# Earlier slots and tile-by-tile sends in a routed feed-forward stage, with two dense steps moved behind the row tiles

## The reference

```python
def _L1_ffn_ref(x, ln_gamma, ln_beta, router_w, gate_up_w, down_w, shared_gate_up_w, shared_down_w):
    normed = (xt - mu) * jax.lax.rsqrt(var + LN_EPS) * ln_gamma + ln_beta
    probs = jax.nn.softmax(normed @ router_w.T, axis=-1)
    top_v, top_i = jax.lax.top_k(probs, 2)
    gates = jax.nn.softmax(top_v, axis=-1)
    comb = jnp.sum(jax.nn.one_hot(top_i, E) * gates[..., None], axis=1)
    for e in range(E):
        out = out + comb[:, e, None] * _swiglu(normed, gate_up_w[e], down_w[e])
    return out + _swiglu(normed, shared_gate_up_w, shared_down_w)
```

## Time and profile before

| | us |
|---|---|
| median of 3 runs | 321.09 |
| lowest, highest | 319.01, 323.36 |
| the profiled execution's own time | 319.61 |
| its span, first to last instruction | 317.8 |
| PE busy | 268.3 (84%) |
| DVE busy | 236.4 (74%) |
| ACT busy | 204.4 (64%) |
| POOL busy | 158.9 (50%) |
| mean granted TensorE clock | 0.941 |

### The profile page before, as it was taken

One profiled execution on the slowest core, in us unless ns is written; L12 is line 12 of the kernel. 1 busy time (PEld: TensorE's weight loads), 2 busy tenths in 40 slices (PEclk: granted clock), 3 DMA queues, 4 the chain that ended last, 5 costly groups with the idle time before them and its releaser, 6 DMA issues.

```text
span 317.8 us, 7526 instructions
## 1 busy us (share of the span) xinstructions
PE 268.3 (84%) x2406; PEld 201.9 (64%) x2406; DVE 236.4 (74%) x711; ACT 204.4 (64%) x469; POOL 158.9 (50%) x206
## 2 busy tenths in 40 slices
PE   7878986997999797999988853878899999999950
PEld 4553442555677464676766732368799999999940
DVE  3586198857977666788999967998576767677796
ACT  2964799796577588976855543535657575756560
POOL 2624297024622546643024777770047878787531
PEclk9999999899999999999999655879999999999995
DMA  7890003001269999970000011113122223111064
GB/s 211 233 383 10 1 2 132 0 3 19 117 188 185 178 181 180 190 105 0 2 1 24 30 45 40 53 49 88 37 71 68 78 67 87 51 32 33 8 226 132
DMA packets 34612, 28.12 MB, mean 88 GB/s; under 512 B 3072, under 2 KB 32389, under 8 KB 33936
## 3 DMA queue, kind: packets, MB, share of 16 engines
q1 hardware_dynamic: 32192, 23.77, 33.8%
q0 software_dynamic: 2240, 3.72, 3.6%
q10 hardware_dynamic: 144, 0.15, 0.2%
HBM read 14.15 MB, written 14.40 MB: 90 GB/s over the span
## 4 chain that ended last, share of the span: by engine, by line
PE 52%; DVE 30%; ACT 8%; issue 6%; DMA 2%; SPq 1%; POOL 1%; DVEq 0%
PE bank L1195 47%; DVE region_k L912 2%; DVE region_x L1152 2%; DVE top L911 2%; DMA wr<-in 2%; PE bank L1492 1%; DVE bn_raw L870 1%; DVE nm L1001 1%; DVE region_k L1003 1%; DVE x L1141 1%; DVE x L1142 1%; ACT x_hat L540 1%; DVE x L902 1%; PE bank L1419 1%; DVE region_k L969 1%
## 5 line engine op out<-in xcount | busy, mean ns | idle before, releaser
L1177 DVE TENSOR_TENSOR region_k<-region_x,region_k 128x768 f16<-128x768 f32 (+1 forms) x33 | 30.6, 926 | 21.6 <-ACT region_k L714 21.6
L1195 PE MATMUL bank<-w_high,region_k 128*128 (+1 forms) x380 | 37.8, 221 | 6.4 <-DVE x L1171 3.3
L1195 PE MATMUL bank<-w_scaled,w_high 128*128 128x256 f16 x252 | 42.5, 273 | 0.1
L846 POOL DMA_INDIRECT expert_rows<-region_k,slot_dest x22 | 27.1, 1232 | 26.5 <-DVE region_k L1164 19.2
L714 ACT ACTIVATE region_k<-region_x 128x768 f16<-128x768 f32 (+1 forms) x33 | 26.8, 813 | 15.8 <-DVE region_x L1152 13.7
L820 POOL DMA_INDIRECT dispatched_rows<-region_t,slot x28 | 28.8, 1028 | 16.1 <-issue 8.3
L1195 PEld LDWEIGHTS bank<-w_high,region_k 128*128 128x128 f16 x380 | 30.9, 99 | 7.7 <-issue 7.3
L1195 PE MATMUL bank<-w_scaled,w_low 128*128 128x256 f16 x126 | 34.3, 273 | 0.0
L1195 PE MATMUL bank<-w_low,region_k 128*128 (+1 forms) x190 | 34.0, 221 | 0.0
L1152 DVE SCALAR_TENSOR_TENSOR region_x<-bank,region_w 128x768 f32<-128x768 f32 (+1 forms) x33 | 30.4, 920 | 3.2 <-ACT region_w L719 2.2
L1195 PE MATMUL bank<-filler 128*128 128x512 f16 x94 | 26.9, 407 | 3.9 <-DVE region_k L912 2.4
(11 more groups left out here) (242 smaller groups left out, 736.1 us busy)
## 6 DMA issues: line engine op xcount, KB each, us to landing
dispatched_rows<-pad_rows SPq DMA_DIRECT2D x8, 1048.0 KB, 18.8
w_scaled<-in SPq DMA_DIRECT2D x5, 1024.0 KB, 8.0
w_scaled<-dispatched_rows SPq DMA_DIRECT2D x21, 131.0 KB, 2.3
region_q<-expert_rows SPq DMA_DIRECT2D x3, 512.0 KB, 5.0
x<-in SPq DMA_DIRECT2D x4, 256.0 KB, 4.4
region_w<-in SPq DMA_DIRECT2D x2, 512.0 KB, 7.0
out<-x SPq DMA_DIRECT2D x3, 256.0 KB, 2.3
w_scaled<-in SPq DMA_DIRECT2D x1, 704.0 KB, 4.1
```

The lines of the kernel that those rows point to most:

```text
L846: pool.indirect_dma_start(ytok, bass.IndirectOffsetOnAxis(dst[:, n, h:h + 1].bitcast(U32), 0), yv[n % 4][:, h * D:(h + 1) * D], None, boun ...
L1177: dve.tensor_tensor(hsplit[:, v, k:2 * k], hid[:, v, 0:k], hsplit[:, v, 0:k], ALU.subtract).then_inc(hidden_low, 1)
L1195: return pe.matmul(o, l, r, start=start, stop=stop)
```

## The change

Four things, and with them the line numbers of the changed kernel are a few higher than those before (L1135 becomes L1140, L1152 becomes L1157, L1167 becomes L1172, L820 becomes L826).

1. `DENSE_FIRST` goes from 3 to 1: the rows steps are steps 5 to 25 instead of 7 to 27, and seven dense steps follow them instead of five. The 33 steps are the same ones.
2. On DVE the `slots` of the first two groups come directly behind the place where their ranks are made.
3. POOL's sends are four stages of one tile each instead of two of two, and their places move; `rstd2` of the last two groups stands among them.
4. At the end ACT scales tiles 8 to 11 before its last 16-bit copy, tiles 4 to 7 move from DVE to ACT and POOL, DVE sums its four tiles as 1, 2 and 1, and SP's loads and stores come in another order.

```diff
-DENSE_FIRST = 3
+DENSE_FIRST = 1
...
-C_POOL = {"rstd": -4.6, "early_low": -5.3, "low": -0.9, "rstd2": 6.5, "send": 12.5, "send2": 16.1}
+C_POOL = {"rstd": -4.6, "early_low": -5.3, "low": -0.9, "rstd2": 6.5, "send0": 11.3, "send1": 11.32, "send2": 11.34, "send3": 11.36}
...
-            for g in (0, 2, 1, 3):
+            for g in (2, 0, 1, 3):
                 n = slice(*GROUPS[g])
                 eng.dma_start(yk[:, n, :], ytok_v[:, n, :]).then_inc(x_loaded[g], 16)
-            for g, ready, count in ((2, last_added, 2), (0, sum_done, T), (SPARSE, rows_ready, len(STEPS)), (3, last_added, 4),
-                                    (1, sum_done, 2 * T)):
+            for g, ready, count in ((2, last_added, 2), (0, sum_done, T), (1, last_added, 4), (3, last_added, 6),
+                                    (SPARSE, rows_ready, len(STEPS))):
...
+            def gated_rows(g):
+
+                act.wait_ge(gates_done, 1)
+                act.wait_ge(x_loaded[g], 32)
+                for c in range(2):
+                    for t in range(*GROUPS[g]):
+                        last = act.activation(yk[:, t, c * D:(c + 1) * D], yk[:, t, c * D:(c + 1) * D], ACT.Copy,
+                                              scale=gate[:, t, c:c + 1])
+                    last.then_inc(last_gated, 1)
...
+                if s == len(STEPS) - 2:
+                    gated_rows(2)
...
-            for g in (2, 3):
-                act.wait_ge(x_loaded[g], 32)
...
+            gated_rows(1)
+            gated_rows(3)
...
-                elif stage == "send" and g is not None and g < SPARSE:
-                    pool.wait_ge(padded, 16 * (E + 2))
...
-                    send_rows(range(lo, lo + 2))
-                elif stage == "send2" and g is not None and g < SPARSE:
-                    send_rows(range(lo + 2, hi))
+                elif stage[:4] == "send" and g is not None and g < SPARSE and lo + int(stage[4]) < hi:
+                    if stage == "send0":
+                        pool.wait_ge(padded, 16 * (E + 2))
+                        pool.wait_ge(slots_ready, g + 1)
...
+                    send_rows(lo + int(stage[4]))
...
-            for k, (g, c) in enumerate(((2, 0), (2, 1), (3, 0), (3, 1))):
+            for k, (g, c) in enumerate((g, c) for g in (2, 1, 3) for c in range(2)):
...
-                    sum_rows(range(1, 4))
-            dve.wait_ge(x_loaded[1], 32)
-            sum_rows(range(4, 8))
+                    sum_rows(range(1, 3))
+            sum_rows(range(3, 4))
```

More of the change, by code:

```diff
@@ L99 @@
             ("norm2", 15): 21.9, ("high", 15): 22.1, ("turn_out", 15): 22.3}
-C_DVE_AT = {("affine", 13): 20.8, ("low", 13): 21.0, ("route", 11): 21.4, ("slots", 11): 21.6,
+C_DVE_AT = {("slots", 3): 14.25, ("slots", 7): 18.35, ("affine", 13): 20.8, ("low", 13): 21.0, ("route", 11): 21.4, ("slots", 11): 21.6,
             ("affine", 15): 22.0, ("low", 15): 22.1, ("route", 13): 22.2,
             ("route", 15): 22.5, ("slots", 13): 22.9}
-C_POOL_AT = {("rstd2", 13): 19.4, ("rstd2", 15): 21.5, ("send2", 7): 21.6, ("send", 11): 21.7, ("send2", 11): 21.8, ("send", 13): 21.9}
+C_POOL_AT = {("rstd2", 13): 18.5, ("send0", 7): 18.4, ("send1", 7): 18.6, ("send2", 7): 18.7, ("rstd2", 15): 21.3, ("send3", 7): 21.4,
+             **{(f"send{k}", t): t + 10.5 + 0.1 * k for t in (11, 13) for k in range(4)}}
 FILL_LOAD, FILL_NORM, FILL_CROSS, FILL_SELECT, FILL_ROUND = 10, 4, 2, 3, 4
@@ L724, in _ @@
                     act.activation(gone[:, :], gdif[:, :], ACT.Tanh, scale=0.5).then_inc(top2_tanh, 1)
-            act.wait_ge(gates_done, 1)
-            for g in (2, 3):
-                act.wait_ge(x_loaded[g], 32)
-                for c in range(2):
-                    for t in range(*GROUPS[g]):
-                        last = act.activation(yk[:, t, c * D:(c + 1) * D], yk[:, t, c * D:(c + 1) * D], ACT.Copy,
-                                              scale=gate[:, t, c:c + 1])
-                    last.then_inc(last_gated, 1)
+            gated_rows(1)
+            gated_rows(3)
         @block.gpsimd
```

14 lines of the change are left out of this document (6 added, 8 removed).

## The result

The changed kernel takes **323.76 us** (median of 20 runs, 321.27 to 328.22) beside 320.94 of the kernel before (20 runs, 318.91 to 323.36): a ratio of **1.0079, 95% interval 1.0049 to 1.0110**, or 2.5 us more (2.5 = 0.0079 x 320.94). Medians and ranges here are of all runs; the ratios leave out runs that lie more than 1.5% above the fastest of the same kernel, here 4 of the 20. The forecast was 323.7. The profiled execution took 324.04 us, its span is 322.2 where that of before is 317.8: 4.4 more. Where these 4.4 are is read from four landmarks. The first operation of the slots of group one stands at 165.50; in before the same place is 164.71. The last silu of ACT starts at 305.34; in before at 301.94.

A forecast was written before the change was run, and what follows sets the result against it. From 225 us on, PE working without a gap was taken as the bound; the profiled execution's 319.61 + 3.1 (entry) + 1.5 (clock) - 0.5 (end) gave 323.7 us, range 319.0 to 327.0.

The forecast's parts named there:

- the entry: Going into the rows steps, DVE and then PE wait for the first row tile: +3.1 us, bounds 1.7 to 5.5.
- the clock: PE's granted clock falls to half speed behind the wait for the first row tile: +1.5 us, bounds 0 and 1.7.
- the end: Behind the last matmuls, the rearranged scalings, adds, sums and stores finish earlier: -0.5 us, bounds -2.2 and +0.6.
- sends in time: Rival: POOL's last send ends at 208.8, the row tile lands when DVE asks, total 319.1 us; chance 0.08.
- POOL's stand: POOL waits 2.9 us ahead of its ninth send for the slots of group two, losing most of its 3.8 lead.
- sends gain nothing: Rival: POOL's last send still ends at 213.8, a wait for the row tile of 5.5 us, total 326.1; chance 0.10.
- a fall is likelier than not: PE's granted clock probably drops to 1.2 GHz after the wait for the first row tile, costing 1.5 us.
- the clock holds: Rival: PE's clock does not fall in the wait for the first row tile, total 322.2 us; chance 0.24.
- some 4 us: Forecast time PE stands from 213.6 to 218.0, but for one turn, waiting for the first row tile.
- I take it at its 0.96: DVE's last low half (L1177) takes 0.96 us, not held by POOL's add; if held, 0.6 more.
- PE's last `down` (by 310.5 even at 1.2 GHz) is covered: PE's last `down` is done by 310.5, hidden behind DVE's sums and SP's stores, so it adds no time.
- The tail is freer: Rival: DVE's last sums slip between POOL's adds at 0.34 each, last store 2.2 earlier, total 320.5 us; chance 0.18.

The follow-up runs named there:

- e9: Changed kernel plus 22 matmuls of 256 columns nobody reads, 12 ahead of the first row tile's turn on PE and 10 behind it: 325.19 us, ratio 1.0107.
- e10: Changed kernel with ACT's eight scalings of tiles 8 to 11 moved back behind its last copy: 324.23 us, ratio 1.0119.
- e12: Changed kernel plus 46 matmuls of 256 columns nobody reads, on PE ahead of its last `down`: 323.37 us, ratio 1.0100.
- e1: Kernel before with DENSE_FIRST = 1 and nothing else: 328.19 us, ratio 1.0217.
- e4: Changed kernel with the piece of tiles 0 to 3 stored last instead of second: 323.03 us, ratio 1.0047.
- e7: Changed kernel with DVE's sum of the first token tile moved behind the last product's dense result: 324.57 us, ratio 1.0114.
- e5: Changed kernel with PE's `down` of step 3 ahead of the first turn and DVE's first destination made one step later: 325.18 us, ratio 1.0108.
- e8: Kernel before with the new order of slots, norms and sends and one dense step in front, keeping the old end: 322.27 us, ratio 1.0016.
- e13: Kernel before with the new order of slots, norms and sends, plus 5 unread matmuls of 512 columns ahead of the first stage's second transposes: 320.79 us, ratio 1.0029.

## Why the forecast came out, and what in it was wrong

The time is right, at 323.76 against 323.7, but only the mechanism of the entry bears it. The rest is luck, twice. The error in the clock (+1.5 forecast, 0 in the profiled execution) and that in the end (-0.5 forecast, +1.0 measured) cancel. And the forecast added 4.1 us to one execution of 319.61 that lay 1.3 below the median of 20 runs; added to the median of 321.09 that was known then it would have been 325.2. The change itself measured 2.5 us, not 4.1.

**The sends and the entry: right in mechanism, 0.5 to 1.5 too high.** The first send 1.9 behind the slots, POOL's stand, the last send's end and the order of waits are as forecast; the rival "sends in time" fell with POOL's gap, "sends gain nothing" with last sends that end 46.0 to 47.6 behind the slots against 49.1. The entry is +2.6 in the profiled execution and +1.6 in e9, e10 and e12, instead of +3.1. In the profiled execution SP's first read came 1.76 behind the last send where the earlier trace rows had 2.35, 0.6 less, and the last send ended 0.2 later. What it has above the 1.6 of the others are 0.9 of three sends at 205 to 211 us that took 1.20, 1.41 and 1.19 instead of 0.96 in the changed kernel and 0.96 in e10. What slowed them isn't shown.

**The clock, +1.5: right in size, wrong as the usual case.** That was the step "a fall is likelier than not". It fell in the profiles of e1, e4 and e7 and held in those of the changed kernel, e5, e8, e10 and e12 (e9 was filled): the rival "the clock holds" described the usual execution. Part of the error is the length of the wait, "some 4 us". PE stood 2.96 in the changed kernel, 2.0 or less in e8, e10 and e12, and 3.9 and 5.4 in e4 and e1, where the clock fell. The length alone does not decide it, as e7 stood only 1.8 and lost its clock.

**The end, -0.5: wrong, it is +1.0.** Two steps failed. "I take it at its 0.96" (L1177, now L1182): the row showed it alone, and next to POOL's add it took 1.64. Here the rule that the prediction set against it (the Trainium skill, SBUF — State Buffer, "Who interferes with whom": a DVE instruction with two inputs in SBUF and a GpSimd instruction that reads SBUF block each other, the one that comes second waiting) holds, 0.7 by this trace; e8 and e10, where no add runs at that time, show 0.96. And "PE's last `down` (by 310.5 even at 1.2 GHz) is covered": it could start only when DVE had taken the dense result before it, which stood behind two sums held by POOL; it began at 314.23 at a clock of 0.50, and DVE waited 0.53 for it. e7 and e12 each give back 0.65 of this. POOL's adds ended 9.7 behind the last silu, exactly as forecast (311.6 - 301.94); the last sum came 12.26 behind it instead of 11.0. That is 1.3 of the 1.5 by which the end was wrong; the other 0.3 is the span's end behind the last store's issue, 3.0 instead of 2.7, which the sum had as unchanged; the slowest store lands 2.8 after its issue instead of 2.4. The 1.6 of the four stores in a row was right, and it is the largest single cost in the end: e8, with the same last sum and one store behind it, ends 1.9 earlier, and e4 takes 1.1 of it away. "The tail is freer" fell with 1.35 and 1.37.

**The front, 0: +0.8 in this execution.** The clock fell at 12 to 15 us. The sum 317.8 + 0.8 + 2.6 + 1.0 = 322.2 is the profiled span. On the medians the +1.6 to +2.6 of the entry and the +1.0 of the end make 2.6 to 3.6, and 2.5 (1.6 to 3.5) was measured.

## What to carry to other kernels

A step that is moved to the end of a program pays only if what follows it is not the bound there: follow the last result of the slow engine through every instruction queued ahead of it, before calling it covered. A result that the slow engine finishes last should have one store behind it, not four: that order cost more here than all that was won by moving sums. An add on POOL beside two-input work on DVE lengthens the DVE instruction that the chain needs; released behind it, as in e10, the adds let the last sum end 1.1 earlier, though no time here shows that gain. A gain of a microsecond is read from landmarks of the trace that lie between what varies; the median of 6 or 12 runs that spread over 4 us doesn't show it.

## What the runs showed of the hardware that was not expected

- The first 24 us differ most between the profiles. In five of the fourteen one small DMA lands late and holds one ACT instruction for 1.4 to 2.15 us, PE stands for 2.0 to 2.7 us, the granted clock goes to 0.50 for some microseconds, and everything behind is 2.4 us later or more (first slots at 167.5 to 168.6 instead of 163.6 to 165.1). That this makes the spread of one kernel's runs is likely and not shown: there is one trace of each kernel, and e13 did not shrink the spread. Moving that tanh behind the norms was not tried.
- The wait at the entry, cut by one turn of four transposes, is not equally long in each execution. PE stood 5.4 and 3.9 us in two profiles, and the granted clock fell to 0.50 behind it (e1, e4); it stood 1.1 to 3.0 us in five and the clock held (the changed kernel, e5, e8, e10, e12), and 1.8 us in one where it fell (e7). With matmuls in the wait that nobody reads the clock stayed at 1.00 in the two profiles that had them (e9, e12's end).
- ACT's scalings are not lengthened by POOL's adds as DVE's sums are: 0.30 us each in both pieces, the eight from 306.05, of which a good half lies ahead of the adds, and the twelve from 309.12 beside them.
